# Two graph layers on one core: node tiles of 128 in place of 125, another order of the work in the preparation and the first edge stage, and no gathers of padding

## The chip, the cores and the metric

The kernel runs on one core of one Trainium2 chip. The metric is the device time of one execution in microseconds (us). A core has five engines with an instruction stream each: TensorE (PE, its weight loads are listed as PEld), VectorE (DVE), ScalarE (ACT), GpSimd (POOL) and SyncE (SP). They meet only at semaphores.

## What is computed

`x` has 6250 nodes of 256 values; 100,000 edges, sorted by `dst`, carry 64 values each. Two layers follow each other:

```python
h = relu(layernorm(x))
# layer 0, with a loop edge of zeros at every node
e   = relu(edge_attr @ ee_w1 + ee_b1) @ ee_w2 + ee_b2
agg = segment_sum(h[src] + e, dst)
y   = (1 + eps) * h + agg
y   = relu(ln(y @ w1 + b1)); y = relu(ln(y @ w2 + b2)); y = y @ w3 + b3
x   = x + relu(ln(h + y))
# layer 1, attention with 8 heads of 32, loops included
hp    = relu(layernorm(x)) @ W + b
s     = leaky_relu(h_src[src] + h_trg[dst])
alpha = exp(s - max(s)) / (segment_sum(exp(s - max(s)), dst) + 1e-10)
out   = x + segment_sum(hp[src] * alpha, dst)
```

Here `h_src` and `h_trg` are the sums of `hp * a_src` and `hp * a_trg` over a head. The second matrix of the edge network is applied after the sum over edges, per node.

## The kernel before

Nodes are cut into 50 tiles of 125 (`TN`, `NT`). Edges are cut into batches of 512 (`BE`), each in four chunks of 128; 100,000 edges fill 195.3 batches, and `NB` = 196. A table made in the preparation tells for every batch the first node tile that its `dst` reach and one past the last. A batch whose edges reach two tiles is called a straddling batch here; its sums are made twice, once for each tile. As `dst` is sorted, there is one such batch at every border between tiles.

The program has five parts.

- **`prepare`** normalises `x` in ten groups of five tiles (`PG`), writes the table of gathered rows to memory as a high and a low f16 half (`tab0`), turns the nodes' own part into `acc`, and makes the schedule. DVE does the statistics (L325, L328), the coefficients (L333, L334), the low halves (L346) and, in every second group, one half of the own part (L341); ACT normalises (L252), makes the high halves (L261) and takes the rest of the own part (L268); POOL adds a bias (L228); SP stores. `numbers`, `own_factors` and `schedule` are small DVE jobs that are slipped in between the groups. The buffers `tb` hold three groups, and `high` waits until a buffer has been stored.
- **`edges0`**, the first edge stage. For every batch POOL issues four gathers of 128 table rows (L550) into a ring of six buffers (`DEEP`). A round of POOL waits for `rows_free` once it is six batches ahead. The edge network of a batch goes through all engines: ACT copies the edge values to f16 (`eab`, L560, and `eah`, L561) and, after that, a part of the copy into a free corner of the network's own buffer in PSUM (L566); DVE makes the low part out of it (L665); PE multiplies (L612, L613: eight matmuls into `mlp_ps`); ACT takes the activation (`rh`, L587); DVE makes its low half (`rl`, L697). Then PE multiplies the gathered rows, `rh` and `rl` with a one-hot matrix of the batch's `dst` (L626, L627: 32 matmuls into `sum_ps`) and DVE adds the result to `acc` (L674). `hot` (L425) is the one-hot matrix. PE's body for batch b issues the edge network's matmuls of batch b+1 first and the sums of batch b after them; where b straddles, the second sums follow. PE loads its tile numbers from the table once in six batches, DVE once in four (both L436). After every sixteen batches ACT and DVE prepare one row of the node network's weights (L573, L576, L758, L749, L753).
- **`nodes`** runs the node network tile after tile, as a pipeline over five tiles, on f16 halves (L979); it writes the second table (`tab1`).
- **`edges1`**, the second edge stage, gathers `tab1` rows (L1561) into a ring of eight and sums them by one-hot matrices.
- **`finish`** divides by the sums of the exponents. Three of the ten groups of five tiles are scaled by ACT, head by head (L1934), the others by DVE.

In the first edge stage the order of the work is written out by hand. On ACT one turn is

```python
high_parts(1 - s)      # L560, L561, L566 of batch b+1
act.wait_ge(mlp_done, 1)
act.wait_ge(r_free, 1)
act.activation(rh...)  # L587 of batch b
```

`mlp_free` lets ACT write into the corner of the PSUM buffer once DVE has read that buffer's last batch; `r_free` lets ACT overwrite `rh` and is given by DVE's `used`, which stands after `add` and, behind a straddling batch, after `add_extra` (L687). DVE's function `advance` does the low part of batch b+1, the low half of batch b, the sums of batch b-1 and the one-hot matrix of batch b+1.

Of the kernel before, what the change touches and what calls it, by code (L numbers as in the profile page):

```python
# [32 lines left out]
P = 128  # L33
N, D, E, ED, H = 6250, 256, 100000, 64, 1024
TN = 125
NT = N // TN
# [5 lines left out]
NCH = NBP * CB  # L42
KH, KD = H // P, D // P
# [13 lines left out]
def build(nc, t, out):  # L57

    with ExitStack() as ctx:
        keep = Memory(nc, ctx)  # L60
        dram = {
            "tab0": nc.dram_tensor("tab0_scratch", (N, 2 * D), F16, kind="Internal").ap(),
            "tab1": nc.dram_tensor("tab1_scratch", (N, TW), F32, kind="Internal").ap(),
            "x1": nc.dram_tensor("x1_scratch", (N, D), F32, kind="Internal").ap(),
# [47 lines left out]
def prepare(nc, t, dram, sb):  # L112


    with ExitStack() as ctx:
# [3 lines left out]
        CH = NT // PG  # L119
        HALF = 112  # L120
        TB = 3
# [19 lines left out]
        tb = m.sb("tb", [TN, TB, PG, 2 * D], F16)  # L141
# [24 lines left out]
        tb_stored = [m.sem(f"tb_stored{s}") for s in range(TB)]  # L166
# [6 lines left out]
        def tiles(c):  # L173
            return slice(c * PG, (c + 1) * PG)
# [7 lines left out]
        def _(sp):  # L182
# [12 lines left out]
            def store(c):  # L195
                sp.wait_ge(tb_ready, c + 1)
                for rows in splits:
                    sp.dma_start(tb_v[rows, tiles(c), :], tb[rows, c % TB]).then_inc(tb_stored[c % TB], 16)

            for c in range(CH - 1):  # L200
                store(c)
            sp.wait_ge(sched_ready, 1)
            sp.dma_start(dram["spans"][1:NBP + 1].rearrange("(p j) c -> p (j c)", j=2), spans_sb[:].rearrange("p j c -> p (j c)")).then_inc(stored, 16)
            sp.dma_start(dram["spans"][0:1], spans_sb[0:1, 0, :]).then_inc(stored, 16)
            for p in range(2):
                line = dram["sched"][p]
                sp.dma_start(line[1:NBP + 1].rearrange("(p j) -> p j", j=2), sched_sb[:, p, :]).then_inc(stored, 16)
                sp.dma_start(line[0:1].unsqueeze(0), sched_sb[0:1, p, 0:1]).then_inc(stored, 16)
            store(CH - 1)
            sp.wait_ge(stored, 112)  # L210
            for s in range(TB):
                sp.wait_ge(tb_stored[s], 32 * len(range(s, CH, TB)))

        @block.gpsimd
        def _(pool):
# [8 lines left out]
            for c in range(CH):  # L224
# [3 lines left out]
                pool.tensor_tensor(ht[:, c % 2], acc[0:TN, tiles(c), 0:D], b2bc[:].unsqueeze(1).broadcast_to([TN, PG, D]),  # L228
# [6 lines left out]
        def _(act):  # L235
# [12 lines left out]
            def normalised(c):  # L248
                act.wait_ge(coef_ready, c + 1)
                for k in range(c * PG, (c + 1) * PG):  # L250
# [4 lines left out]
            def high(c):  # L255
                act.wait_ge(t_ready, c + 1)
# [4 lines left out]
                act.activation(tb[:, c % TB, :, 0:D], ht[:, c % 2], ACT.Copy).then_inc(hi_ready, 1)  # L261

            def own(c):
                if c == 0:
                    act.wait_ge(own_coef, 1)
                for j in range(KD) if on_act(c) else (0,):
                    act.wait_ge(own_done[j], c + 1)
                    act.activation(accT[:, tiles(c), j, 0:TN], own_ps[j][:, 0:PG, 0:TN], ACT.Identity,  # L268
# [5 lines left out]
            for c in range(CH + 3):  # L274
# [15 lines left out]
                if c == 5:  # L290
# [5 lines left out]
        def _(pe):  # L296
# [7 lines left out]
            for c in range(CH):  # L304
                pe.wait_ge(tb_ready, c + 1)
                for j in (1, 0):
                    if c:
                        pe.wait_ge(own_kept[j], c)
                    for k in range(PG):
# [6 lines left out]
        def _(dve):  # L316
# [5 lines left out]
            def stats(c):  # L322
                dve.wait_ge(ld_x[c], 32)
                for k in range(c * PG, (c + 1) * PG):
                    ins = dve.bn_stats(stat[:, k, :], acc[0:TN, k, 0:D])  # L325
                settled(ins)
                for k in range(c * PG, (c + 1) * PG):
# [9 lines left out]
            def own(c):  # L337
# [3 lines left out]
                dve.tensor_scalar(accT[:, tiles(c), 1, 0:TN], own_ps[1][:, 0:PG, 0:TN], eps2[:], own_off[:, 1:2],  # L341
                                  ALU.mult, ALU.add).then_inc(own_kept[1], 1)

            def low(c):
                dve.wait_ge(hi_ready, c + 1)
                settled(dve.tensor_tensor(tb[:, c % TB, :, D:2 * D], ht[:, c % 2], tb[:, c % TB, :, 0:D], ALU.subtract))  # L346
# [3 lines left out]
            def extremes(j):  # L350
                dve.wait_ge(ld_dst, 16)
                dve.tensor_reduce(ext[:, j:j + 1], drow[:, j, :], AX, ALU.min)
# [1667 lines left out]
```

## Time and profile before

| | us |
|---|---|
| median of the three runs (lowest to highest) | 3133.91 (3132.59 to 3136.23) |
| the profiled execution's own time | 3134.97 |
| its span, from the first to the last instruction | 3133.0 |
| PE busy | 2456.0 |
| DVE busy | 2233.0 |
| POOL busy | 1984.4 |
| ACT busy | 1592.6 |

The profiled execution lies 1.06 us above the median. The busy times are sums over four stages that differ in kind, so none of them is the bound by itself. The preparation ends at 89 us, the first edge stage at 1122 us, the node stage at 2089 us; the second edge stage and the last part take the rest. The start of an instruction in a timeline is the moment at which its waits were over.

### The profile page before, as it was taken

The numbers are of one execution on the slowest core, as the hardware profiler recorded it, in microseconds if no ns is written. First come the engines' busy times: TensorE is split into PE (matmuls) and PEld (weight loads), VectorE is DVE, ScalarE is ACT, GpSimd is POOL, SyncE is SP. The second block draws the span as 40 slices with busy tenths as digits, with TensorE's granted clock in tenths as the row PEclk, the third lists the DMA queues.
The fourth block names the chain that finished last, engine by engine and source line by source line (L and its number), as shares of the span: only waits on it lengthen the run. The fifth ranks groups of instructions, "written<-read, shape, count | busy, mean of one in ns | idle before, by whom it ended". The sixth has DMA issues, their size and how long they took to land. (4 is left out here: it accounts for less than half of the span.)

```text
span 3133.0 us, 88320 instructions
## 1 busy us (share of the span) xinstructions
PE 2456.0 (78%) x29338; PEld 2164.5 (69%) x29339; DVE 2233.0 (71%) x3932; ACT 1592.6 (51%) x3967; POOL 1984.4 (63%) x2094
## 2 busy tenths in 40 slices
PE   2677677777777779999999999938777777777773
PEld 2566666666666679999999999936555555555652
DVE  6566667776777657777777777758777777777777
ACT  6555555555555558888888888821111111111114
POOL 5677767777777724454544444437777777777772
PEclk9988889888899989999999999969888888988896
DMA  7555555555555510000000000026555555555554
GB/s 168 165 152 160 152 147 159 164 162 160 158 157 160 148 45 17 23 20 21 23 20 21 20 23 20 23 77 178 172 173 170 171 174 174 167 174 172 172 171 135
DMA packets 183986, 373.55 MB, mean 119 GB/s; under 512 B 42741, under 2 KB 93959, under 8 KB 183912
## 3 DMA queue, kind: packets, MB, share of 16 engines
q0 software_dynamic: 75552, 209.45, 23.7%
q1 hardware_dynamic: 107392, 162.37, 17.2%
q10 hardware_dynamic: 968, 0.87, 0.1%
q8 instruction: 31, 0.51, 0.1%
q14 instruction: 43, 0.35, 0.0%
HBM read 346.95 MB, written 25.80 MB: 119 GB/s over the span
## 5 line engine op out<-in xcount | busy, mean ns | idle before, releaser
L550 POOL DMA_INDIRECT rows<-tab_scratch,srcs x784 | 750.7, 958 | 264.4 <-issue 229.3
L1561 POOL DMA_INDIRECT a_rows<-tab_scratch,srcs x784 | 751.7, 959 | 250.9 <-issue 226.7
L1627 PE MATMUL sum_ps<-feat,a_hot 128*125 128x264 f32 x1960 | 599.0, 462 | 207.1 <-DVE feat L1720 98.1
L1627 PEld LDWEIGHTS sum_ps<-feat,a_hot 128*125 128x125 f32 x1960 | 417.6, 222 | 310.3 <-issue 117.8
L979 PE MATMUL z_ps<-ah,w 128*128 128x125 f16 x6400 | 555.1, 219 | 2.7 <-PEq L1075 2.6
L979 PE MATMUL z_ps<-al,w 128*128 128x125 f16 x3200 | 544.1, 218 | 0.0
L979 PEld LDWEIGHTS z_ps<-ah,w 128*128 128x128 f16 x6400 | 490.8, 97 | 3.5 <-issue 3.4
L1571 ACT ACTIVATE feat<-d 128x32 f32<-128x32 f32 x196 | 44.9, 229 | 827.2 <-DVE d L1716 580.5
L626 PE MATMUL sum_ps<-hot,rows 128*128 128x125 f16 x1960 | 356.1, 235 | 53.0 <-PEq L642 24.6
L612 PE MATMUL mlp_ps<-ewa,eab 128*128 128x256 f16 x788 | 213.9, 301 | 229.6 <-PEq L608 229.1
L626 PE MATMUL sum_ps<-hot,rh 128*128 128x125 f16 x1960 | 354.4, 234 | 0.0
L627 PE MATMUL sum_ps<-hot,rows 128*128 128x125 f16 x1960 | 354.3, 234 | 0.0
L627 PE MATMUL sum_ps<-hot,rl 128*128 128x125 f16 x1960 | 354.1, 234 | 0.0
L942 POOL TENSOR_TENSOR a<-a 128x500 f32<-128x500 f32 x100 | 153.8, 1538 | 310.8 <-POOLq L941 310.8
L1134 ACT ACTIVATE a<-z,pack 128x125 f32<-128x125 f32 x800 | 316.7, 483 | 44.2 <-ACTq L1132 44.2
L979 PEld LDWEIGHTS z_ps<-al,w 128*128 128x128 f16 x3200 | 315.6, 99 | 0.4
L612 PEld LDWEIGHTS mlp_ps<-ewa,eab 128*128 128x128 f16 x788 | 84.6, 107 | 265.1 <-issue 250.1
L626 PEld LDWEIGHTS sum_ps<-hot,rows 128*128 128x128 f16 x1960 | 205.9, 106 | 87.7 <-issue 84.2
L697 DVE SCALAR_TENSOR_TENSOR rl<-mlp_ps,rh 128x1024 f16<-128x1024 f32 x196 | 240.0, 1225 | 34.0 <-DVEq L696 29.6
L665 DVE TENSOR_TENSOR eab<-ea,mlp_ps 64x512 f16<-64x512 f32 x197 | 136.2, 691 | 164.4 <-DVEq L664 160.0
L566 ACT ACTIVATE mlp_ps<-eab 64x512 f32<-64x512 f16 x197 | 117.5, 597 | 250.7 <-ACTq L565 238.4
L1720 DVE TENSOR_TENSOR feat<-a_rows,p_ps 128x1024 f32<-128x1024 f32 x196 | 239.2, 1220 | 3.9 <-DVEq L1507 0.5
(220 smaller groups left out, 5938.7 us busy)
## 6 DMA issues: line engine op xcount, KB each, us to landing
ea<-edge_t SPq DMA_DIRECT2D x394, 128.0 KB
dstb<-dst_flat SPq DMA_DIRECT2D x98, 512.0 KB, 4.0
rows<-tab_scratch,srcs POOLq DMA_INDIRECT x784
a_rows<-tab_scratch,srcs POOLq DMA_INDIRECT x784
tab_scratch<-prow SPq DMA_DIRECT2D x50, 128.9 KB
hx<-x SPq DMA_DIRECT2D x50, 125.0 KB
x_scratch<-x SPq DMA_DIRECT2D x50, 125.0 KB
hs<-tab_scratch SPq DMA_DIRECT2D x50, 125.0 KB
```

The source lines that it names most:

```text
L550: pool.indirect_dma_start(rows[:, b % DEEP, k, :], None, dram["tab0"], bass.IndirectOffsetOnAxis(ap=srcs[:, c:c + 1], axis=0),).then_inc(r ...
L612: pe.matmul(mlp_ps[:, s, k, :], eab[:, s, e], ewa[:], start=True, stop=False)
L626: pe.matmul(to, high, rhs, start=(k == 0 and q == 0), stop=False, skip_group_check=True)
L627: ins = pe.matmul(to, low, rhs, start=False, stop=(k == CB - 1), skip_group_check=True)
L665: dve.tensor_tensor(eab[ED:P, s, :], ea[ED:P, s, :], high_ps[s], ALU.subtract).then_inc(ea_split, 1)
L697: dve.scalar_tensor_tensor(out=rl[:, s].rearrange("p k d -> p (k d)"), in0=mlp_ps[:, s].rearrange("p k d -> p (k d)"), scalar=0.0, in1=rh[ ...
L942: settled(pool.tensor_tensor(a[j][:, 0:4, :], a[j][:, 0:4, :], a[j][:, 4:8, :], ALU.add))
L979: ins = pe.matmul(out, lhs, rhs, start=(k == 0 and q == 0), stop=(k == n - 1 and q == 2))
L1134: ins = act.activation(a[j][:, k, :], z[j][:, k, :], ACT.Relu, bias=cols[be][:, k:k + 1], scale=cols[g][:, k:k + 1])
L1561: pool.indirect_dma_start(rows[:, b % DEEP, k, :], None, dram["tab1"], bass.IndirectOffsetOnAxis(ap=srcs[:, c:c + 1], axis=0),).then_inc(r ...
L1627: ins = pe.matmul(out[:], hot[:, h, k, :], feat[:, row, k, :], start=(k == 0), stop=(k == CB - 1))
L1720: return dve.tensor_tensor(feat[:, u, :, 0:D].rearrange("p k (h f) -> p k h f", h=HEADS), slot_of(slot)[:, :, 0:D].rearrange("p k (h f) -> ...
```

## The change

Nodes are now cut into 49 tiles of 128; the last has 106 nodes and 22 places without a node, and the inputs and tables are padded to 6272 rows. The preparation, the node stage and the last part count 49 tiles; the last group has four. In the second edge stage the extra partition that caught the padding edges is no longer needed, nor is a fiftieth tile's own loop term, which had been done ahead of the others. The two chunks that hold only padding (783 and 784 of 784) are no longer gathered. In the preparation `numbers` and `own_factors` stand ahead of the first statistics, DVE does the own part after the next statistics, the buffers for table groups lie in the node network's weights' room and number nine, the last bias is added by DVE, and the schedule is made and stored before the last groups. In the first edge stage ACT takes the activation of batch b before the copies of batch b+1, and DVE takes the low half of batch b before the low part of batch b+1.

```diff
-TN = 125
-NT = N // TN
+TN = P
+NT = -(-N // TN)
+TAIL = N - (NT - 1) * TN
+FILLED = -(-E // P)
...
# edges0, POOL (edges1 alike)
-                for k in range(CB):
+                for k in range(min(CB, FILLED - CB * b)):
...
# edges0, ACT
                 act.activation(eab[:, s, :], ea[:, s, :], ACT.Copy).then_inc(eab_chain, 1)
-                act.activation(eah[0:ED, s, :], ea[0:ED, s, :], ACT.Copy).then_inc(eah_done, 1)
                 act.wait_ge(mlp_free, 1)
...
                 act.activation(high_ps[s], eab[ED:P, s, :], ACT.Copy).then_inc(ea_high, 1)
+                act.activation(eah[0:ED, s, :], ea[0:ED, s, :], ACT.Copy).then_inc(eah_done, 1)
...
                 for u in range(RING):
                     s = u % 2
-                    high_parts(1 - s)
                     act.wait_ge(mlp_done, 1)
...
                     act.activation(rh[:, s]...).then_inc(r_high, 1)
+                    high_parts(1 - s)
...
# edges0, DVE, advance
                     extra_hot(b - 1, end - 1)
+                    low_activations(s)
+                    low_parts(1 - s)
                     add(1 - s, lo)
-                    low_parts(1 - s)
-                    low_activations(s)
                     main_hot(b + 1, 1 - s, following)
                     add_extra(end - 1)
...
                 with dve.Else():
+                    low_activations(s)
                     low_parts(1 - s)
-                    low_activations(s)
                     add(1 - s, lo)
...
# prepare, DVE
+            numbers()
+            own_factors()
             stats(0)
             for c in range(CH + 3):
                 if c < CH:
                     coefficients(c)
-                if 3 <= c < CH:
-                    own(c - 3)
+                if c == CH:
+                    last_sum()
                 if 2 <= c < CH + 2:
                     low(c - 2)
...
                 if c + 1 < CH:
                     stats(c + 1)
-                if c == 0:
-                    own_factors()
-                if c == 1:
-                    numbers()
+                if c >= 3:
+                    own(c - 3)
...
# prepare, ACT
-                    act.wait_ge(tb_stored[c % TB], 32 * (c // TB))
+                    act.wait_ge(first_stored, 32)
...
# finish, ACT
-                for k in range(i * FB, (i + 1) * FB):
+                for k in range(i * FB, min((i + 1) * FB, NT)):
```

**ACT in the first edge stage.** One turn and the start of the next before the change (`mlp_ps<-eab` is the copy into the corner of PSUM):

```order
L560 ACTIVATE eab<-ea 128x512 [waits ea_ready1]
L561 ACTIVATE eah<-ea 64x512
L566 ACTIVATE mlp_ps<-eab 64x512 [waits mlp_free,eab_chain]
L587 ACTIVATE rh<-mlp_ps 128x1024 [waits mlp_done,r_free]
L560 ACTIVATE eab<-ea 128x512 [waits ea_ready0]
```

And now:

```order
L607 ACTIVATE rh<-mlp_ps 128x1024 [waits mlp_done,r_free]
L582 ACTIVATE eab<-ea 128x512 [waits ea_ready0]
L587 ACTIVATE mlp_ps<-eab 64x512 [waits mlp_free,eab_chain]
L588 ACTIVATE eah<-ea 64x512
L607 ACTIVATE rh<-mlp_ps 128x1024 [waits mlp_done,r_free]
```

The activation `rh` of a batch moved from behind the three copies of the next batch to ahead of them, and the copy into `eah` moved behind the copy into PSUM.

**DVE in the first edge stage, behind a straddling batch.** From the extra one-hot matrix to the addition of the extra sums, before:

```order
L425 SCALAR_TENSOR_TENSOR hot<-dsts,negbase,e_iota_ps 128x500
L674 ISA [waits e_chain,sum_done]
L674 TENSOR_TENSOR acc<-acc,sum_ps 128x4x125
L665 TENSOR_TENSOR eab<-ea,mlp_ps 64x512 [waits ea_high]
L697 SCALAR_TENSOR_TENSOR rl<-mlp_ps,rh 128x1024 [waits r_high]
L425 ISA
L425 SCALAR_TENSOR_TENSOR hot<-dsts,negbase,e_iota_ps 128x500
L687 ISA [waits xsum_done]
L687 TENSOR_TENSOR acc<-acc,sum_ps 128x4x125
```

And now:

```order
L447 SCALAR_TENSOR_TENSOR hot<-dsts,negbase,e_iota_ps 128x512
L718 SCALAR_TENSOR_TENSOR rl<-mlp_ps,rh 128x1024 [waits r_high]
L686 TENSOR_TENSOR eab<-ea,mlp_ps 64x512 [waits ea_high]
L695 ISA [waits e_chain,sum_done]
L695 TENSOR_TENSOR acc<-acc,sum_ps 128x512
L447 ISA
L447 SCALAR_TENSOR_TENSOR hot<-dsts,negbase,e_iota_ps 128x512
L708 ISA [waits xsum_done]
L708 TENSOR_TENSOR acc<-acc,sum_ps 128x512
```

The low half `rl` and the low part `eab` moved ahead of the instruction that waits for the sums of the batch before (`sum_done`), and `rl` now stands first.

**DVE at the start of the preparation.** Before:

```order
L384 MEMSET lneps 128x1
L325 BN_STATS stat<-acc 125x6 [waits p_dve_chain,ld_x0]
L325 BN_STATS stat<-acc 125x6 x4
L328 BN_AGGR mv_ps<-stat 125x2 [waits p_dve_chain]
L328 BN_AGGR mv_ps<-stat 125x2 x4
```

And now:

```order
L406 MEMSET lneps 128x1
L377 TENSOR_SCALAR ident<-idiag 128x128 [waits p_dve_chain,iotas]
L378 TENSOR_SCALAR ident<-idiag 128x128
L379 CAST iota<-icol 128x128
L380 CAST negbase<-ineg 128x49
L381 CAST nodeid<-inode 128x49
L382 CAST thr<-ithr 128x48
L386 TENSOR_SCALAR ecol<-ecol 128x2 [waits p_dve_chain,ld_eps]
L387 TENSOR_SCALAR eps<-eps 128x1
L388 TENSOR_SCALAR ecol<-ecol,eps 128x2 [waits p_dve_chain]
L389 TENSOR_SCALAR eps<-eps 128x1 [waits p_dve_chain]
L339 BN_STATS stat<-acc 128x6 [waits p_dve_chain,ld_x0]
```

The six instructions of `numbers` and the four of `own_factors` moved from behind the statistics of the second and third group to ahead of the first group's.

## Rows read from the trace of the kernel before

**Rows 1.** The first three stages; columns: us, busy of each engine, clock, DMA, GB/s.

```profile
0.00:89.00 89.00, 25.29 (x208) 21.68 (x209) 59.21 (x159) 53.84 (x90) 41.97 (x23) 1.00 0.69 163
89.00:1122.00 1033.00, 752.04 (x9416) 665.28 (x9416) 715.71 (x923) 562.31 (x811) 751.63 (x785) 0.89 0.54 156
1122.00:2089.00 967.00, 927.19 (x14416) 919.31 (x14416) 673.98 (x1169) 796.75 (x2151) 438.52 (x502) 0.98 0.07 22
```

**Rows 2.** Gather instructions of both edge stages, by source line; start times in us.

```profile
L550 POOL DMA_INDIRECT rows<-tab_scratch,srcs x784: 947/953/1744, 90.1 to 1104.1; - x196
...
L1561 POOL DMA_INDIRECT a_rows<-tab_scratch,srcs x784: 952/957/1322, 2089.6 to 3079.5; - x196
```

**Rows 3.** Timeline, batches 95 to 98; columns: start, length in us, engine, line, operation.

```profile
603.39 0.22 PE L626 MATMUL sum_ps<-hot,rows 128*128 128x125 f16 x1 [0.25 <-PEq L642]
...
605.11 0.22 PE L627 MATMUL sum_ps<-hot,rl 128*128 128x125 f16 x1
...
605.97 0.63 ACT L560 ACTIVATE eab<-ea 128x512 f16<-128x512 f32 x1 [0.89 <-ACTq L559]
...
608.66 0.27 PE L612 MATMUL mlp_ps<-ewa,eab 128*128 128x256 f16 x1 [3.33 <-PEq L608]
...
609.26 0.60 ACT L566 ACTIVATE mlp_ps<-eab 64x512 f32<-64x512 f16 x1 [2.14 <-ACTq L565]
...
609.91 1.02 ACT L587 ACTIVATE rh<-mlp_ps 128x1024 f16<-128x1024 f32 x1
...
610.00 0.69 DVE L665 TENSOR_TENSOR eab<-ea,mlp_ps 64x512 f16<-64x512 f32 x1 [1.61 <-DVEq L664]
...
611.09 1.23 DVE L697 SCALAR_TENSOR_TENSOR rl<-mlp_ps,rh 128x1024 f16<-128x1024 f32 x1 [0.40 <-DVEq L696]
```

**Rows 4.** Timeline of ACT at the end of a round of sixteen batches.

```profile
539.44 1.02 ACT L587 ACTIVATE rh<-mlp_ps 128x1024 f16<-128x1024 f32 x1 [0.74 <-ACTq L586]
540.48 1.15 ACT L573 ACTIVATE centred<-w,wneg 128x1024 f32 x1
541.82 1.06 ACT L576 ACTIVATE w<-centred 128x1024 f32 x1 [0.19 <-ACTq L575]
```

**Rows 5.** Timeline, batch 101, matmuls twice as long.

```profile
629.28 0.69 DVE L665 TENSOR_TENSOR eab<-ea,mlp_ps 64x512 f16<-64x512 f32 x1 [2.26 <-DVEq L664]
...
630.26 0.36 PE L612 MATMUL mlp_ps<-ewa,eab 128*128 128x256 f16 x1 [4.94 <-PEq L608]
...
632.32 1.02 ACT L587 ACTIVATE rh<-mlp_ps 128x1024 f16<-128x1024 f32 x1
```

**Rows 6.** Register loads of the schedule in the first edge stage, by source line.

```profile
L436 PEldq TENSOR_LOAD <-st x66: 1003/1466/1662, 98.2 to 1105.4; - x66
```

**Rows 7.** Timeline of DVE in the same place.

```profile
538.21 0.67 DVE L687 TENSOR_TENSOR acc<-acc,sum_ps 128x500 f32 x1
...
543.16 1.24 DVE L758 TENSOR_TENSOR w<-centred,w 128x1024 f32 x1
...
548.27 0.69 DVE L665 TENSOR_TENSOR eab<-ea,mlp_ps 64x512 f16<-64x512 f32 x1 [2.25 <-DVEq L664]
```

**Rows 8.** Timeline, the first matmul of the first edge stage.

```profile
97.72 0.37 PE L612 MATMUL mlp_ps<-ewa,eab 128*128 128x256 f16 x1 [11.56 <-PEq L608]
```

**Rows 9.** Timeline of the preparation, POOL and DVE.

```profile
6.98 5.42 POOL L222 MEMSET acc<- 128x6400 f32 x1
...
8.82 1.73 DVE L325 BATCH_NORM_STATS2 stat<-acc 125x6 f32<-125x256 f32 x5 [7.94 <-DMA acc<-x]
...
21.82 2.98 DVE L362 CAST thr<-ithr 128x49 f32<-128x49 int32 x1
...
74.99 3.96 DVE L346 TENSOR_TENSOR tb<-ht,tb 125x1280 f16<-125x1280 f32 x1 [0.75 <-ACT tb L261]
```

**Rows 10.** One operation of each node tile, by source line.

```profile
L1128 ACT ACTIVATE a<-z x50: 1029/1037/1041, 1131.5 to 2023.2; 128x1000 f32<-128x1000 f32 x50
```

**Rows 11.** Timeline of ACT in the last stage.

```profile
3101.53 25.54 ACT L1934 ACTIVATE acc<-acc,f_g 125x32 f32<-125x32 f32 x120 [3.71 <-DVEq L1970]
```

More of the change, by code:

```diff
@@ L165, in prepare @@
         own_kept = [m.sem(f"own_kept{j}") for j in range(KD)]
-        tb_stored = [m.sem(f"tb_stored{s}") for s in range(TB)]
+        first_stored, tb_stored, t_last = m.sem("first_stored"), m.sem("tb_stored"), m.sem("t_last")
         dve_chain = m.sem("p_dve_chain")
@@ L223, in _ @@
             pool.wait_ge(ld_b2, 16)
-            for c in range(CH):
+            for c in range(LASTC):
                 pool.wait_ge(norm_ready, c + 1)
@@ L249, in normalised @@
                 act.wait_ge(coef_ready, c + 1)
-                for k in range(c * PG, (c + 1) * PG):
+                for k in range(c * PG, c * PG + count(c)):
                     h = acc[0:TN, k, 0:D]
@@ L255, in high, with own @@
             def high(c):
-                act.wait_ge(t_ready, c + 1)
+                if c < LASTC:
+                    act.wait_ge(t_ready, c + 1)
+                else:
+                    act.wait_ge(t_last, 1)
                 if c >= TB:
-                    act.wait_ge(tb_stored[c % TB], 32 * (c // TB))
+                    act.wait_ge(first_stored, 32)
                     for j in range(KD):
                         act.wait_ge(own_done[j], c - TB + 1)
-                act.activation(tb[:, c % TB, :, 0:D], ht[:, c % 2], ACT.Copy).then_inc(hi_ready, 1)
-            def own(c):
+                act.activation(tb[:, c % TB, 0:count(c), 0:D], ht[:, c % 2, 0:count(c)], ACT.Copy).then_inc(hi_ready, 1)
+            def own(c, parts):
                 if c == 0:
                     act.wait_ge(own_coef, 1)
-                for j in range(KD) if on_act(c) else (0,):
+                for j in parts:
                     act.wait_ge(own_done[j], c + 1)
-                    act.activation(accT[:, tiles(c), j, 0:TN], own_ps[j][:, 0:PG, 0:TN], ACT.Identity,
+                    act.activation(accT[:, tiles(c), j, 0:TN], own_ps[j][:, 0:count(c), 0:TN], ACT.Identity,
                                    bias=own_off[:, j:j + 1], scale=eps2[:]).then_inc(own_kept[j], 1)
@@ L286, in _ @@
                 if c >= 3:
-                    own(c - 3)
+                    own(c - 3, (1,) if on_act(c - 3) else (0,))
                 if c + 1 < CH:
                     deviation(c + 1)
-                if c == 5:
+                if c >= 3 and on_act(c - 3):
+                    own(c - 3, (0,))
+                if c == 6:
                     act.wait_ge(eb_split, 1)
@@ L308, in _ @@
                         pe.wait_ge(own_kept[j], c)
-                    for k in range(PG):
+                    for k in range(count(c)):
                         out = own_ps[j][:, k, 0:TN]
@@ L323, in stats @@
                 dve.wait_ge(ld_x[c], 32)
-                for k in range(c * PG, (c + 1) * PG):
+                for k in range(c * PG, c * PG + count(c)):
                     ins = dve.bn_stats(stat[:, k, :], acc[0:TN, k, 0:D])
                 settled(ins)
-                for k in range(c * PG, (c + 1) * PG):
+                for k in range(c * PG, c * PG + count(c)):
                     ins = dve.bn_aggr(mv[:, k, :], stat[:, k, :])
@@ L633, in _, with body @@
             edge_mlp(0)
-            def body(tiles, i, u):
+            def body(tiles, i, u, last=False):
                 s = u % 2
@@ L643, in body @@
                 pe.sem_inc(mlp_free, 1)
-                pe.wait_ge(rows_ready[u], 16 * CB * (i + 1))
+                pe.wait_ge(rows_ready[u], 16 * (CB * (i + 1) - (NB * CB - FILLED if last else 0)))
                 sums(sum_ps[:, s, :], s, u, s).then_inc(sum_done, 1)
@@ L885, in bodies @@
         def bodies(eng, body):
-            first, last = 4, NT - 2
+            first, last = 4, NT - 3
+            assert (last - first) % 2 == 0
             for i in range(first):
@@ L1558, in _ @@
                     pool.wait_ge(rows_free, b - DEEP + 1)
-                for k in range(CB):
+                for k in range(min(CB, FILLED - CB * b)):
                     c = CB * b + k
@@ L1915, in _ @@
         def _(sp):
-            out_v = out.rearrange("(t p) c -> p t c", p=TN)
+            whole = (NT - 1) * TN
+            out_v = out[0:whole].rearrange("(t p) c -> p t c", p=TN)
             for i in range(steps):
-                tiles = slice(i * FB, (i + 1) * FB)
+                tiles = slice(i * FB, min((i + 1) * FB, NT - 1))
                 sp.wait_ge(out_ready, i + 1)
@@ L1921, in _ @@
                     sp.dma_start(out_v[rows, tiles, :], acc[rows, tiles, 0:D]).then_inc(out_stored, 16)
-            sp.wait_ge(out_stored, 32 * steps)
+            sp.dma_start(out[whole:N], acc[0:TAIL, NT - 1, 0:D]).then_inc(out_stored, 16)
+            sp.wait_ge(out_stored, 32 * steps + 16)
         @block.scalar
```

129 lines of the change are left out of this document (70 added, 59 removed).

## The prediction

> **What bounds the kernel now.** I read the windows by stage first, because the stages differ in kind. The preparation takes 89 us, the first edge stage 1033, the node stage 967 with PE busy in 927 of them [rows 1]; what is left of the span (3133.0) is 1044 us. No engine is full in the first edge stage: PE is busy in 752 of 1033 us. Then I read the gathers [rows 2]. In the second edge stage 784 of them start over 989.9 us, one each 1.264 us, with little else to do. In the first edge stage they start over 1014.0 us, one each 1.295. At the second stage's pace a batch of four could come every 5.06 us; it came every 5.18. So the gathers are close to being the pace, but the computation holds them up a little. The reader should see there a stage with a slack of some 2% in either direction: a loop of more than 5.06 us per batch on the compute side lengthens it, and a shorter one gains 784 × (1.295 − 1.264) = 24 us and a part of the 18 that follow the last gather (1104.1 to 1122).
>
> Then I read the timeline of single batches. Now, ACT copies the edge values of batch b+1 (L560, L561, L566) while PE and ACT are still busy with batch b; the next network's inputs are ready early, and the activation `rh` comes after them. This is a pipeline of two batches. The example shows also what disturbs it: the last sums matmul of a batch starts at 605.11, and PE's next network matmul only at 608.66, 3.55 us later, of which PE stood idle for 3.33 [rows 3]. PE loads its tile numbers in between.
>
> **The first edge stage: a serial loop.** After the change ACT does `rh` of b first and then copies for b+1. `rh` of b waits for the network's matmuls of b, these for the low part of b on DVE, this for ACT's copy into PSUM of b, and this stands in ACT's queue behind `rh` of b−1. The dependence goes round once per batch, and nothing in it overlaps:
>
> - network matmuls to `rh`: 608.66 to 609.91, 1.25 us [rows 3];
> - `rh` to ACT's next instruction: 539.44 to 540.48, 1.04 us [rows 4];
> - copy `eab`: 0.63 long [rows 3], and the next instruction of ACT that waits for the one before stands 0.19 more [rows 4]: 0.82 us;
> - copy into PSUM to low part: 609.26 to 610.00, 0.74 us [rows 3];
> - low part to network matmul: 629.28 to 630.26, 0.98 us [rows 5].
>
> The sum is 4.83 us at 2.4 GHz. What lies beside it: `rl` of b starts 1.18 us behind `rh` and lasts 1.23 [rows 3], 2.41 in all, and the low part is due 1.04 + 0.82 + 0.74 = 2.60 behind it, so `rl` hides; the sums of one batch take 603.39 to 605.33 = 1.94 [rows 3], and with the network's matmuls, which are over within the 1.25, they fit in 4.83, and the columns from 125 to 128 hide with them. `eah` and the additions hide too. 196 × 4.83 = 947, and 4 for the tail. Alone this is under 5.06, and the gathers would decide. But a serial loop never catches up: whatever holds one batch up is added in full, where the old pipeline took it beside the copies. I count four such things.
>
> (a) PE's registers: 66 loads of 1.47 us in pairs [rows 6], 32 times in the stage. PE's own loop is there the network, the sums, the loads: from the first sums matmul to the next network 603.39 to 608.66 = 5.27 [rows 3], and ahead of it the network, about 0.89 as an estimate (the 1.25 without the last matmul's 0.27 and some 0.09 for the signal): 6.16 instead of 4.83, +1.3. In 14 of the 32 the batch or the one before straddles (counted from `dst` with tiles of 128; 7 with tiles of 125), which puts 1.72 more on PE (603.39 to 605.11): +3.0. 18 × 1.3 + 14 × 3.0 = 65 us.
>
> (b) The other 34 of the 48 straddling batches (49 before): `r_free` comes only behind `add_extra`, 538.21 + 0.67 to `rh` at 539.44, 0.56 us [rows 4, 7], and `add_extra` waits for second sums. About 0.9 each: 31 us. Nearest bounds: nothing, and 1.72.
>
> (c) Twelve weight rows: from DVE's product on a row to the next low part pass 543.16 to 548.27, 5.1 us [rows 7], with ACT's two instructions 2.4 [rows 4] ahead. The old pipeline covered much of it. I take 5.0 each: 60 us; the lower bound is ACT's 2.4, 29 us.
>
> (d) The clock. It was 0.89 on average [rows 1], so (1 − 0.89)/0.5 = 22% of the stage at 1.2 GHz. There, network to `rh` is 630.26 to 632.32 = 2.06 [rows 5], 0.81 more than at 2.4 GHz. I keep a fifth: 0.2 × 196 × 0.81 = 31 us; bounds 0 and 159.
>
> The stage begins 8.7 us ahead of its first network matmul (89 to 97.72 [rows 8]). Sum: 8.7 + 951 + 65 + 31 + 60 + 31 = 1147, against 1033: **+114 us**. With the least that I can defend of (a) to (d), 93 us ((a) 32 × 1.3 = 42, (c) 29, (d) 22, (b) nothing), it is +20; with (a) and (b) at 1.72 more for each straddle, (c) with 2.4 more and (d) at half of the stage, about +200. I take the middle terms, because each has its row in this stage.
>
> **The preparation.** `thr` takes 2.98 beside POOL's work, and `low` 3.96 once, where a buffer was late [rows 9]; both leave the chain of groups. The own part goes behind the next statistics and the schedule's stores start before the last groups; no row prices these, and I put them at one `low`, 4. Against it, `numbers` and `own_factors` now stand ahead of the first statistics, which started at 8.82, and POOL's memset runs until 12.40 [rows 9]; they could be held until then, +3.6. That is −7, from −14 (nothing held, both moves worth twice as much) to +4 (only the hold counts). The DVE instructions there that are long for their size end with POOL's, as the rows suggest. The Trainium skill ("GPSIMD Engine Reference", § 1. Specifications) says that GpSimd shares an SBUF interface with VectorE; by it the ten small instructions would be drawn out under the memset, and the preparation would come out at about +3 instead of −7, the kernel at 3244.
>
> **Nodes.** 50 tiles pass at (2023.2 − 1131.5)/49 = 18.2 us [rows 10], PE being the bound. One tile fewer is −18.2; if each tile cost 128/125 as much, 49 × 18.6 = 913 against 910, +3. PE does most work in blocks of 512 columns, and a part by the tile's columns. I take −3.
>
> **Second edge stage and finish.** 782 gathers of 1.264 instead of 784 [rows 2]: −2.5. ACT scales 14 tiles by 8 heads, 112 operations instead of 120, each 25.54/120 = 0.213 [rows 11]: −1.7; bounds 0 and −3.
>
> **Sum.** 114 − 7 − 3 − 2.5 − 1.7 = +99.8. The profiled execution has 3134.97 and lies 1.06 above the median: 3134.97 + 99.8 − 1.06 = 3233.7, **3234 us**.
>
> **The rivals.** *A, faster: the gathers set the pace.* If most of (a) to (d) falls in time in which the batch waits for its rows anyway, a mean batch takes under 5.06 us, and (782 × 1.264 = 988) + 9 us of start and tail make the stage 997, −36; with the other gains (−14) the kernel takes about 3084. The place is the loop's 4.83, the point is disturbances of less than 0.23 × 196 = 45 us in all. For it speaks that the loop alone is under the gathers' pace; against it that (a) alone, which the trace shows bare in the old order, makes 42 to 65.
> *B, nothing:* the lower bounds of (a) to (d) hold: +20 − 14 = +6 on the median: 3140. With (d) at nothing too it is 22 less, with the preparation's gain gone 8 more.
> *C, slower still: the clock falls more.* In a loop with longer pauses for PE the low clock's share may go from a fifth to half or more: 0.3 × 196 × 0.81 = 48 more by this loop alone, and more with the sums: about 3300. Rows show that both levels occur in this stage [rows 1, 5]. The Trainium skill ("TensorE: Matmul & The Clock Gate", "Loop structure matters more than you think") says that PE work in dense stretches keeps the clock and long waits between lose it; by it the change, which spaces the stretches out, leads to case C.
> *D:* that a step doesn't do what is said is excluded by the order lists, which show ACT's and DVE's new order.
>
> **How the numbers follow.** A 0.15, B 0.12, C 0.06, the forecast 0.67, with its own range 3165 to 3290. Within 0.2% (6 us, about what a measurement of this kernel can tell from no change) lies only a part of B, which I spread from 3100 to 3165: 0.05 there, 0.05 below it and 0.02 above. Faster: A and that lower part, 0.20. Slower: the forecast, C and the upper part, 0.75. The range, 3095 to 3300, takes in the forecast's own range, the whole of B, the near third of A and the near half of C; two thirds of A (0.10), the far half of C (0.03) and 0.05 of the forecast remain outside.
>
> **What would show it.** Right: after the change the windows by stage give the first edge stage about 1147 us; ACT's `rh` of consecutive batches stands 4.8 us apart where nothing disturbs; POOL waits long for free rows. Wrong: POOL without waits, gathers one each 1.27 us, and a stage under 1010 (case A); or a spacing of `rh` well off 4.83. In the node stage 49 tiles at 18.5 us or so; in the preparation the first statistics at about 12 us instead of 8.82.

## The result, and the profile after the change

The changed kernel takes 3264.86 us (median of four runs, 3262.53 to 3267.17) against 3133.25 us before (four runs): a ratio of 1.0421, 95% interval 1.0403 to 1.0439. That is +131.6 us where +100 was forecast. The profiled execution has 3262.53 us and a span of 3260.7, 127.7 more than the span before.

The windows by stage of the changed kernel, with the columns of [rows 1]:

```profile
0.00:80.00 80.00, 24.44 (x204) 21.63 (x205) 63.80 (x158) 52.45 (x89) 38.27 (x22) 1.00 0.74 181
80.00:1257.00 1177.00, 797.89 (x9384) 723.99 (x9384) 733.52 (x921) 568.20 (x811) 751.04 (x783) 0.84 0.47 137
1257.00:2218.00 961.00, 916.69 (x14128) 885.57 (x14128) 674.75 (x1147) 790.38 (x2108) 445.92 (x492) 0.98 0.07 22
2218.00:3260.00 1042.00, 746.83 (x5278) 561.17 (x5278) 783.36 (x1676) 176.34 (x900) 748.47 (x783) 0.84 0.58 170
```

The first edge stage has grown from 1033 to 1177 us, and its clock has fallen from 0.89 to 0.84; every other stage is shorter. From here on, the stage is taken from its first gather to the end of its last addition: 90.1 to 1121.9 before (1031.8 us) and 81.1 to 1257.0 now (1175.9), +144.1. The other parts: the preparation −9.0 (first gather at 81.1, at 90.1 in [rows 2]), the node stage 961.7 instead of 967.7, −6.0, the second edge stage with the finish 1042.1 instead of 1043.5, −1.4. The sum is +127.7.

The gathers, by source line, with what POOL waited for in the first stage (us, times):

```profile
L572 POOL DMA_INDIRECT rows<-tab_scratch,srcs x782: 947/953/1996, 81.1 to 1230.1; - x196
...
  DVEq L699: 184.4, 74
...
L1584 POOL DMA_INDIRECT a_rows<-tab_scratch,srcs x782: 952/957/1081, 2218.6 to 3204.1; - x196
```

POOL waited 184 us for `rows_free` (L699). In the second stage gathers still start one each 1.262 us ((3204.1 − 2218.6)/781). So the transfers did not become slower; POOL was held up by the computation.

An undisturbed round in the first edge stage, in the timeline of ACT, DVE and PE:

```profile
247.92 1.02 ACT L607 ACTIVATE rh<-mlp_ps 128x1024 f16<-128x1024 f32 x1 [1.77 <-ACTq L606]
...
249.10 1.22 DVE L718 SCALAR_TENSOR_TENSOR rl<-mlp_ps,rh 128x1024 f16<-128x1024 f32 x1 [1.36 <-DVEq L717]
...
249.57 0.60 ACT L587 ACTIVATE mlp_ps<-eab 64x512 f32<-64x512 f16 x1
...
250.35 0.69 DVE L686 TENSOR_TENSOR eab<-ea,mlp_ps 64x512 f16<-64x512 f32 x1
...
251.34 0.27 PE L633 MATMUL mlp_ps<-ewa,eab 128*128 128x256 f16 x1 [1.84 <-PEq L629]
...
252.60 1.02 ACT L607 ACTIVATE rh<-mlp_ps 128x1024 f16<-128x1024 f32 x1 [1.77 <-ACTq L606]
```

The round from `rh` to `rh` is 252.60 − 247.92 = 4.68 us, and 80 of 195 rounds lie between 4.67 and 4.70; before, the shortest round was 3.36. The reader can follow two ways round. By ACT: `rh` to the copy into PSUM 1.65, to the low part 0.78. By DVE: `rh` to `rl` 1.18, to the low part 1.25. Both make 2.43, and after them come the low part to the network, 0.99, and the network to `rh`, 1.26. The low part starts 0.03 us behind the end of `rl` (250.32): the two ways tie.

A round behind a border between tiles (the first matmul of the batch's sums, the extra one-hot matrix, the first matmul of the second sums, the network, the extra addition, `rh`):

```profile
252.23 0.22 PE L647 MATMUL sum_ps<-hot,rows 128*128 128x128 f16 x1
...
253.81 0.75 DVE L447 SCALAR_TENSOR_TENSOR hot<-dsts,negbase,e_iota_ps 128x512 f16<-128x512 f32 x1 [1.39 <-issue]
...
255.52 0.31 PE L647 MATMUL sum_ps<-hot,rows 128*128 128x128 f16 x1
...
257.43 0.27 PE L633 MATMUL mlp_ps<-ewa,eab 128*128 128x256 f16 x1
...
257.83 0.69 DVE L708 TENSOR_TENSOR acc<-acc,sum_ps 128x512 f32 x1
...
259.07 1.02 ACT L607 ACTIVATE rh<-mlp_ps 128x1024 f16<-128x1024 f32 x1 [3.57 <-ACTq L606]
```

Network matmuls would have been due at 251.34 + 4.68 = 256.02. PE does the second sums just ahead of the network, which starts at 257.43, 1.41 us late. In this round the extra one-hot matrix is ready at 253.81 + 0.75 = 254.56, but PE is then still at the batch's own sums, which run at the low level of the clock, 1.2 GHz (0.51 in the stretch below):

```profile
252.30:255.70 3.40, 3.40 (x35) 3.40 (x34) 2.00 (x3) 2.77 (x4) 2.49 (x4) 0.51 0.65 180
```

From the start of the first to the start of the last matmul they take 3.18 us, and 1.73 in most of the 48 rounds behind borders. In 37 of the 48 the order is the other way: PE has done the batch's own sums and stands still for 0.7 us or more until the extra one-hot matrix is there, which DVE mostly makes behind its loads. Then `rh` waits for the extra addition (257.83 + 0.69, and 0.55 more) until 259.07; 1.26 behind the network it would have started at 258.69, so this is 0.38 us. The round shown has 6.47 us, 1.79 more than 4.68. Where PE's loads fall into the same round, such rounds have 9.2 us on average (10 of them), with a weight row 11.4 (6), with both 14.1 (4).

### The profile page after: what moved, and what is told of

Same layout as the page of the kernel before. It is cut to its first block and busy times, and to the rows that moved or that the text cites. A ratio compares the mean times of both kernels' runs of the same rounds, so it can differ in the third digit from the quotient of the medians.

```text
span 3260.7 us, 87292 instructions
## 1 busy us (share of the span) xinstructions
PE 2485.8 (76%) x28994; PEld 2192.4 (67%) x28995; DVE 2255.4 (69%) x3901; ACT 1587.4 (49%) x3907; POOL 1983.7 (61%) x2079
## 5 line engine op out<-in xcount | busy, mean ns | idle before, releaser
L1648 PE MATMUL sum_ps<-feat,a_hot 128*128 128x264 f32 x1952 | 593.4, 461 | 219.1 <-PEq L1535 104.4
L1648 PEld LDWEIGHTS sum_ps<-feat,a_hot 128*128 128x128 f32 x1952 | 424.2, 226 | 317.8 <-issue 190.3
L1000 PE MATMUL z_ps<-ah,w 128*128 128x128 f16 x6272 | 544.2, 220 | 2.0 <-PEq L1096 1.8
L1000 PE MATMUL z_ps<-al,w 128*128 128x128 f16 x3136 | 533.3, 220 | 0.0
L607 ACT ACTIVATE rh<-mlp_ps 128x1024 f16<-128x1024 f32 x196 | 200.3, 1022 | 569.5 <-ACTq L606 536.7
L647 PE MATMUL sum_ps<-hot,rows 128*128 128x128 f16 x1952 | 379.4, 247 | 72.1 <-PEq L670 72.1
L647 PE MATMUL sum_ps<-hot,rh 128*128 128x128 f16 x1952 | 379.2, 247 | 0.0
L648 PE MATMUL sum_ps<-hot,rows 128*128 128x128 f16 x1952 | 379.2, 247 | 0.0
L648 PE MATMUL sum_ps<-hot,rl 128*128 128x128 f16 x1952 | 378.8, 247 | 0.0
L1155 ACT ACTIVATE a<-z,pack 128x128 f32<-128x128 f32 x784 | 312.3, 484 | 40.0 <-ACTq L1153 40.0
L447 DVE SCALAR_TENSOR_TENSOR hot<-dsts,negbase,e_iota_ps 128x512 f16<-128x512 f32 (+1 forms) x245 | 181.6, 743 | 75.6 <-issue 73.5
```

Source lines behind the costliest of these rows:

```text
L447: return dve.scalar_tensor_tensor(out=out, in0=at, scalar=negbase[:, bass.ds(tile, 1)], in1=iota_ps.unsqueeze(1).broadcast_to([P, CB, TN]) ...
L607: act.activation(rh[:, s].rearrange("p k d -> p (k d)"), mlp_ps[:, s].rearrange("p k d -> p (k d)"), ACT.Relu).then_inc(r_high, 1)
L647: pe.matmul(to, high, rhs, start=(k == 0 and q == 0), stop=False, skip_group_check=True)
L648: ins = pe.matmul(to, low, rhs, start=False, stop=(k == CB - 1), skip_group_check=True)
L1000: ins = pe.matmul(out, lhs, rhs, start=(k == 0 and q == 0), stop=(k == n - 1 and q == 2))
L1155: ins = act.activation(a[j][:, k, :], z[j][:, k, :], ACT.Relu, bias=cols[be][:, k:k + 1], scale=cols[g][:, k:k + 1])
```

## The experiments

The theory (S): the new order closes a serial loop of 4.7 us per batch, and this loop, not the gathers, is the pace of the stage. The rivals: with tiles of 128 borders fall into the same batches as DVE's loads (P); DVE's order, with the extra sums behind the low parts, costs the time (D); gathers set or slow the stage (G). Twelve kernels were run. The stage lengths are from the first gather to the last addition of one execution, the profiled one. 1 to 6 were timed four times each, 7 to 12 once, so these have no interval.

| kernel | whole, us | first edge stage, us |
|---|---|---|
| before | 3133.3 | 1031.8 |
| changed | 3264.9 | 1175.9 |
| 1: changed, old order | 3115.0 | 1023.5 |
| 2: before, new order | 3260.6 | 1151.2 |
| 3: changed, old order on ACT only | 3249.1 | 1161.3 |
| 4: changed, old order on DVE only | 3280.0 | 1187.0 |
| 5: changed, PE's loads behind the network | 3255.5 | 1170.4 |
| 6: as 1, PE's loads behind the network | 3091.6 | 998.3 |
| 7: changed, half the gathers | 3260.6 | 1168.0 |
| 8: as 1, half the gathers | 3114.1 | 1017.9 |
| 9: changed, no second sums | 3083.8 | 996.0 |
| 10: changed, no weight rows | 3208.8 | 1117.8 |
| 11: as 8, no second sums | 2852.1 | 755.3 |
| 12: as 7, no second sums | 3084.9 | 992.2 |

**1: the old order back, everything else as changed.**

```diff
 # ACT, high_parts
                 act.activation(eab...).then_inc(eab_chain, 1)
+                act.activation(eah...).then_inc(eah_done, 1)
...
                 act.activation(high_ps[s]...).then_inc(ea_high, 1)
-                act.activation(eah...).then_inc(eah_done, 1)
 # ACT, turn
+                    high_parts(1 - s)
                     act.wait_ge(mlp_done, 1)
...
                     act.activation(rh...).then_inc(r_high, 1)
-                    high_parts(1 - s)
 # DVE, advance at a border
                     extra_hot(b - 1, end - 1)
-                    low_activations(s)
-                    low_parts(1 - s)
                     add(1 - s, lo)
+                    low_parts(1 - s)
+                    low_activations(s)
 # DVE, advance elsewhere
-                    low_activations(s)
                     low_parts(1 - s)
+                    low_activations(s)
                     add(1 - s, lo)
...
```

> The changed kernel with the order of before on ACT and on DVE in the first edge stage; tiles of 128, preparation and gathers as changed. Serial loop (theory S): the first edge stage falls from 1177 us to about 1030, the whole to about 3118 us, below the kernel before, as the other parts gained some 15. Rival P (with 128 nodes a tile holds 2048 edges on average, four batches, so that nearly every border falls into the batches where DVE also loads its tile numbers): that stays, and the stage keeps some 50 us of its 144, 3165 us.

3115.03 us, a ratio to before of 0.9947 (0.9930 to 0.9963). The stage's row:

```profile
81.30:1104.80 1023.50, 735.08 (x9384) 648.74 (x9384) 720.79 (x918) 560.22 (x811) 751.87 (x782) 0.91 0.55 157
```

The stage is 8 us shorter than before, at a clock of 0.91, and the kernel 19 faster. So the order makes the whole loss, and what was changed beside it gains. P's 50 us are not there.

**2: the new order alone in the kernel before**, the reverse of the diff above.

> The kernel before with the changed order on ACT and DVE in the first edge stage alone; tiles of 125, preparation and gathers of before. S: spacing of rh 4.7 us where nothing disturbs, the stage about 1160, the whole about 3255 to 3280 us. P: the order costs only some 90 us, 3220 us, because borders and loads meet only by chance with tiles of 125.

3260.60 us, ratio 1.0406 (1.0386 to 1.0426): in S's range. The order costs 1151.2 − 1031.8 = 119 us of the stage with tiles of 125 and 1175.9 − 1023.5 = 152 with tiles of 128; of the whole, by the medians, it costs 127 and 150. Some 23 to 33 us thus belong to the order and the tiles together. In the changed kernel 44 of the 48 rounds behind borders are also rounds with DVE's loads, with tiles of 125 it is 12 of 49; a tile of 128 nodes has 2048 edges on average, four batches. That this is the reason was not tried by itself.

**3: the old order on ACT only; 4: on DVE only.** Each has its half of the diff of 1.

> The changed kernel with the order of before on ACT alone; DVE as changed. S: the loop is opened by ACT's copies alone, the same time as with both orders put back, within 10 us. Rival D (DVE's order, its extra sums behind the low parts, costs the time): like the changed kernel, about 3250 to 3265 us.

> The changed kernel with the order of before on DVE alone; ACT as changed. S: the loop stays serial, 3265 us or a little more, since low parts now stand ahead of the low half without need. D: about 3120 us.

3249.13 us for the first (1.0365, 1.0347 to 1.0382), 3280.04 for the second (1.0472, 1.0455 to 1.0490). S as I had put it, with ACT alone, falls for 3, where D's figure came, and D falls for 4. A round of each shows why. Old order on ACT:

```profile
247.28 0.60 ACT L588 ACTIVATE mlp_ps<-eab 64x512 f32<-64x512 f16 x1 [0.29 <-ACTq L587]
...
248.11 1.02 ACT L609 ACTIVATE rh<-mlp_ps 128x1024 f16<-128x1024 f32 x1 [0.23 <-ACTq L608]
...
249.29 1.22 DVE L719 SCALAR_TENSOR_TENSOR rl<-mlp_ps,rh 128x1024 f16<-128x1024 f32 x1 [1.57 <-DVEq L718]
...
250.55 0.69 DVE L687 TENSOR_TENSOR eab<-ea,mlp_ps 64x512 f16<-64x512 f32 x1
...
251.54 0.27 PE L634 MATMUL mlp_ps<-ewa,eab 128*128 128x256 f16 x1 [0.43 <-PEq L630]
...
252.98 1.00 ACT L609 ACTIVATE rh<-mlp_ps 128x1024 f16<-128x1024 f32 x1
```

ACT's copy into PSUM is done early, and yet the low part of the next batch waits: DVE has it behind `rl`, `rl` waits for `rh`. The round shown is 4.87 us, the commonest one 4.68. Old order on DVE:

```profile
250.68 1.02 ACT L607 ACTIVATE rh<-mlp_ps 128x1024 f16<-128x1024 f32 x1 [1.75 <-ACTq L606]
...
252.34 0.60 ACT L587 ACTIVATE mlp_ps<-eab 64x512 f32<-64x512 f16 x1
...
253.09 0.69 DVE L686 TENSOR_TENSOR eab<-ea,mlp_ps 64x512 f16<-64x512 f32 x1 [1.46 <-DVEq L685]
...
254.08 0.27 PE L633 MATMUL mlp_ps<-ewa,eab 128*128 128x256 f16 x1 [1.46 <-PEq L629]
...
255.34 1.02 ACT L607 ACTIVATE rh<-mlp_ps 128x1024 f16<-128x1024 f32 x1 [1.74 <-ACTq L606]
```

Here `rl` is out of the way, and the low part waits for ACT's copy. The round is 4.66 us. Each of the two moves closes the loop by itself, at the same length; both have to go.

**5 and 6: PE's loads behind the network**, in the changed kernel and in 1.

```diff
-            def body(tiles, i, u, last=False):
+            def body(tiles, i, u, last=False, n=DEEP):
                 s = u % 2
                 edge_mlp(1 - s)
+                if u == 0:
+                    tiles.extend(tiles_of(nc, PE, table, DEEP * i, n))
...
-                tiles = tiles_of(nc, PE, table, DEEP * i, DEEP)
+                tiles = []
```

> The changed kernel, but PE loads its tile numbers behind the network of the group's first batch instead of ahead of it. If the serial loop is the pace (S), each of the 32 loads, which made a round of rh about 2.5 us longer than 4.68, now lies mostly beside the loop's steps on ACT and DVE: some 50 us less, about 3215 us. If gathers or something else set the pace (rival G): no change, 3265 us.

> The same move of the loads in the changed kernel with the old order on ACT and DVE. If that one's first edge stage (1023 us) is close to the gathers' pace (988 us), at most 25 to 30 us go: 3090 to 3105 us. If it is still the pace of the computation alone, 50 us or more would go.

3255.52 us (1.0405, 1.0388 to 1.0423) and 3091.55 us (0.9883, 0.9867 to 0.9900). For 5 my 50 us were wrong; the stage lost 5.5. One such place in PE's timeline:

```profile
164.18 0.27 PE L633 MATMUL mlp_ps<-ewa,eab 128*128 128x256 f16 x1
...
168.05 0.29 PE L647 MATMUL sum_ps<-hot,rows 128*128 128x128 f16 x1 [2.82 <-PEq L665]
...
171.27 0.27 PE L633 MATMUL mlp_ps<-ewa,eab 128*128 128x256 f16 x1
```

From one network to the next PE now needs 171.27 − 164.18 = 7.09 us, because network, loads and sums stand one behind the other on PE and the sums run at the low level for a part (clock 0.50 from 168 to 171 us). In the changed kernel the first round behind a load, borders and rows apart, had 7.2 us on average; here the second has 6.8. The wait moved one batch on. In 6 the same move gave 25 us of the stage. Its gathers:

```profile
L572 POOL DMA_INDIRECT rows<-tab_scratch,srcs x782: 949/953/1535, 81.3 to 1066.1; - x196
```

They start one each (1066.1 − 81.3)/781 = 1.261 us, the pace of the second stage: of the versions that make all sums, only this one has reached the gathers' floor. It beats the kernel before by 1.2%.

**7 and 8: half the gathers**, in the changed kernel and in 1.

```diff
+            pool.memset(rows[:, :, CB // 2:CB, :], 0.0).then_inc(ones_ready, 1)
...
-                for k in range(min(CB, FILLED - CB * b)):
+                for k in range(CB // 2):
...
```

> The changed kernel with two of four gathers of each batch in the first edge stage; the other two chunks of rows are zeros, so their share of the sums is left out. S: the loop is the pace, the first edge stage keeps its 1176 us within 15. G (gathers set or slow it): well under 1130 us.

> The same with the old order on ACT and DVE. If gathers set its pace for a good part, the stage falls from 1023 us to 900 to 960; if the computation alone does, it stays at 1010 to 1025.

The stage has 1168.0 and 1017.9 us, 8 and 6 less than with all gathers. Of this, 5 us come from the zeros: they are written ahead of the first gather, which starts at 86.6 instead of 81.1 and 81.3. The stage ends 2.5 and 0.4 us sooner. G falls. The second also shows that the gathers do not hold the old order, near as its pace is to theirs.

**9: no second sums at borders; 10: no weight rows.**

```diff
 # 9, PE and DVE
-                with pe.If(end > lo + 1):
-                    with pe.Fori(lo + 1, end):
...
-                with dve.If(end > lo + 1):
...
-                with dve.Else():
 # 10, ACT, DVE and SP
-                row(r)
-                row_mean(r)
-                row_low(r)
-                load_row(r + 1)
```

> The changed kernel without the second sums of a batch that reaches two tiles, in the first edge stage (that part of the sums is left out). By the terms of the prediction (31 us, and 24 in the loads' term) the stage falls by 55 us to about 1120; by the longer rounds of rh that stand two batches behind a border in the changed kernel's trace (some 2 to 2.7 us each) by 100 to 130, to about 1060.

> The changed kernel without the twelve weight rows in the first edge stage (the node network's weights are zeros). By the prediction's term the stage falls by 60 us to about 1116; by the trace (about 4.5 us for a row) by 55.

The stage without second sums, and below without weight rows:

```profile
81.10:1077.10 996.00, 683.70 (x7848) 617.35 (x7848) 671.13 (x822) 568.10 (x811) 748.52 (x782) 0.84 0.55 161
```

```profile
81.30:1199.10 1117.80, 769.98 (x9384) 700.99 (x9384) 701.68 (x882) 544.25 (x787) 765.37 (x783) 0.87 0.48 138
```

Without second sums the stage is 180 us shorter, above even the larger expectation. But 9 leaves out more than the second sums. Nothing reads the last tile of a batch any more, and PE reads no tile number at all; the loads of these numbers are gone too. Below are the changed kernel's loads, and then 9's:

```profile
L458 DVEq TENSOR_LOAD <-st x101: 309/815/833, 81.8 to 1254.1; - x101
L458 PEldq TENSOR_LOAD <-st x66: 1004/1467/1663, 88.1 to 1235.0; - x66
```

```profile
L458 DVEq TENSOR_LOAD <-st x51: 329/807/830, 81.9 to 1075.4; - x51
```

So the 180 us are the price of borders, of PE's loads and of half of DVE's loads together. The rounds of the two traces, batch by batch, divide them: the 34 rounds with a border alone are 2.0 us longer in the changed kernel (69 us), the 17 with PE's loads alone 2.1 (35 us), the 14 with both 4.6 (65 us); the other 130 together make 9. Without weight rows the stage is 58 us shorter, as expected, and the clock is 0.87 instead of 0.84.

**11 and 12: half the gathers and no second sums**, in 1 and in the changed kernel, the edits of 7 and 9 together; PE's loads and half of DVE's are gone here too.

> The changed kernel with the old order on ACT and DVE, with half the gathers (the other rows are zeros) and without the second sums at borders, so that neither gathers nor borders hold its first edge stage. If borders cost the old order about as much as the new one (theory: the change is the longer loop alone), the stage falls from 1018 us to 800 to 880: 196 rounds of 3.4 to 3.9 us, and weight rows and loads. If the old order took the borders beside its copies (the prediction's view), it stays over 960.

> The changed kernel with half the gathers and without the second sums. The serial loop is the floor: 196 x 4.68 = 917 us, weight rows 58 and a little for loads and clock: 975 to 1000, hardly under the 996 us that it took with all gathers. If gathers held that run up, clearly less than 975.

The stage of 11, and below of 12:

```profile
86.50:841.80 755.30, 611.78 (x7848) 521.23 (x7848) 652.96 (x821) 553.88 (x808) 373.58 (x392) 0.95 0.49 144
```

```profile
86.40:1078.60 992.20, 681.20 (x7848) 613.81 (x7848) 669.46 (x820) 566.26 (x808) 373.27 (x392) 0.85 0.39 109
```

Freed of half the gathers, of borders and of PE's loads, the old order needs 755 us and the new one 992: 237 us, weight rows and what is left of DVE's loads included. 9, with all its gathers, has 996; that it is no longer than 12 says that gathers did not hold 9 up either, though they start one each (1066.7 − 81.1)/781 = 1.262 us there. The loop is 196 × 4.68 = 917 us in the new order, and with the 58 of the weight rows 975 of the 992 are accounted for. In the old order a bare round, in the timeline of 11, has 3.36 us, from `rh` at 247.73 to `rh` at 251.09:

```profile
247.73 1.00 ACT L611 ACTIVATE rh<-mlp_ps 128x1024 f16<-128x1024 f32 x1
...
247.94 0.69 DVE L684 TENSOR_TENSOR eab<-ea,mlp_ps 64x512 f16<-64x512 f32 x1 [0.40 <-DVEq L683]
...
248.76 0.63 ACT L584 ACTIVATE eab<-ea 128x512 f16<-128x512 f32 x1
...
248.93 0.27 PE L636 MATMUL mlp_ps<-ewa,eab 128*128 128x256 f16 x1 [0.40 <-PEq L632]
...
250.55 0.60 ACT L590 ACTIVATE mlp_ps<-eab 64x512 f32<-64x512 f16 x1 [0.64 <-ACTq L589]
...
251.09 1.00 ACT L611 ACTIVATE rh<-mlp_ps 128x1024 f16<-128x1024 f32 x1
```

The next batch's low part starts 0.21 us behind `rh`, beside it, and not 2.43 behind, and its network is on PE before `rh` has been over for long.

Borders and loads together cost 1017.9 − 755.3 = 263 us in the old order and 1168.0 − 992.2 = 176 in the new. So the new order does give something back there, 87 us, and 237 − 87 = 150 is what is seen between 7 and 8. By rounds, 8 against 11 and 7 against 12: a border alone costs 3.3 us in the old order and 2.1 in the new, PE's loads alone 2.8 and 2.1, both 5.5 and 4.7. That they cost the old order more because they break a pipeline of two batches is only argued.

## Why the prediction was right, and where it was not

The direction, the range and the likeliest case held, and the sum came to three quarters of what was measured. By its steps:

- **A serial loop.** Right, and it is the cause: putting the order back takes 152 us off the stage. The forecast of 4.83 us was 0.15 too long: `rh` to the copy into PSUM takes 1.65, not 1.04 + 0.82 = 1.86.
- **"`rl` hides".** This failed. It was set against ACT's way of 2.60 us with 2.41; in the run both ways have 2.43. The step saw one loop where there were two, and with either move alone the loop is closed (3 and 4).
- **"Alone this is under 5.06, and the gathers would decide."** This held as far as the runs go: in 9, with the weight rows but without borders and PE's loads, the gathers start at their own pace of 1.262 us.
- **"Where the old pipeline took it beside the copies."** This failed. The old order bears borders and loads as well, with 263 us even more than the new one with 176 (8 and 11, 7 and 12). Its mean round lay near the gathers' pace by coincidence; with half the gathers it stays (8), and without borders and PE's loads the stage falls to 755 us (11). So the computation did not grow by disturbances that the old order had hidden, but by 237 us of longer rounds less 87 that borders and loads cost less. The old order without borders and PE's loads but with all gathers was not run; by the 998 us of 6, as an estimate, the gathers would hold it there, and the longer loop would be hidden, as the text had it.
- **(a) to (d).** Forecast 187 us in all. (c) weight rows: 60 forecast, 58 measured. (a) and (b) together, PE's loads and borders: 65 + 31 = 96 forecast, 180 measured, half of DVE's loads among them (9); these are the terms that were mis-sized. By rounds, loads alone make 2.1 us each where 1.3 was forecast, borders alone 2.0 where 0.9, both 4.6 where 3.0, so that the border is the term that was mis-sized most. Its 0.9 had counted the wait of `rh` for the extra addition, which is 0.38 us in the round shown; 1.41 come from PE, which has the second sums ahead of the next network, there with the batch's own sums at the low level before them. Moving the loads recovers only 5.5 us, as the wait moves with them (5). (d) the clock: 0.84 on average is (1 − 0.84)/0.5 = 32% at 1.2 GHz against 22% before. What this costs by itself was not separated. The networks, from which (d) was reckoned, were hit no more often than before: 33 of the 197 needed over 1.2 us from the start of the first to the start of the last matmul instead of 0.78, and 36 before. The low level comes more often in the sums, as in the border round shown.
- **The sum of the stage**, 1147 forecast for 1177. The size came near partly by luck: the loop's 951 was 30 too many and the clock's 31 have no run that shows them, against 84 too few in (a) and (b).
- **Preparation** −7 forecast, −9.0 measured. The first statistics started at 13.96 us instead of 8.82, later than the 12 that were forecast; the last rows of this document show what held them. The Trainium skill ("GPSIMD Engine Reference", § 1. Specifications) names contention only with VectorE's instructions in a 2-port mode or with two inputs in SBUF, which the prediction left out; in the trace two of the ten small instructions are drawn out and the other eight follow them. The +3 us worked out from that sentence did not come: holds of the same kind, such as `thr`'s 2.98 us inside the chain [rows 9], went at the same time. What each move gave was not separated.
- **Nodes** −3 forecast, −6.0 measured; second edge stage and finish −4.2 forecast, −1.4 measured: its gathers end 4.5 us sooner relative to its start, and what follows the last gather takes 3.1 more. That the last gather is now one of real edges, with its work behind it, would explain this, but it was not tried.
- **Rivals.** A needed rounds under 5.06 us; the mean was 5.94. C, the clock, went its way by a part: the Trainium skill ("TensorE: Matmul & The Clock Gate", "Loop structure matters more than you think") and the stage's mean clock, 0.89 before and 0.84 now, agree in direction, but the low level did not reach half of the stage.

What is open: how much of 144 us the low clock makes by itself, what borders cost without the loads that went with them in 9, 11 and 12, and why borders and loads cost the old order more.

## What to carry to other kernels

When two engines hand a batch back and forth, follow the dependence once round through every engine's queue, in program order: an instruction for batch b+1 that stands behind one for batch b on any of them closes the loop, and undoing it on one engine shows little (15 us either way here) while a second still closes it. A mean pace that agrees with a transfer's pace is no proof that the transfer sets it; halve the transfer and look. And price a rare case (a border) by its whole round, from `rh` to `rh`, and not by the one wait that is easiest to see. Where a part is left out to price it, count the instructions in both traces: what only that part had read is gone with it, and is in the price.

## What was not expected of the hardware

In the changed preparation two small instructions of DVE start while POOL clears `acc`, and last until it is done (the first of them is shown):

```profile
1.62 5.21 POOL L230 MEMSET acc<- 128x6144 f32 x1
...
1.69 10.59 DVE L377 TENSOR_SCALAR ident<-idiag 128x128 f32<-128x128 int32 x1 [0.81 <-POOL ithr L229]
...
6.78 5.42 POOL L231 MEMSET acc<- 128x6400 f32 x1
...
12.27 0.21 DVE L379 CAST iota<-icol 128x128 f16<-128x128 int32 x1
...
13.96 1.73 DVE L339 BATCH_NORM_STATS2 stat<-acc 128x6 f32<-128x256 f32 x5
```

The same instruction in the kernel before, when no memset ran:

```profile
21.25 0.21 DVE L357 TENSOR_SCALAR ident<-idiag 128x128 f32<-128x128 int32 x1
```

So 128 columns took 10.59 us under the memsets and 0.21 without them, while the second memset took 5.42 us in both kernels [rows 9]. Not every instruction of DVE is held: the kernel before did its first five statistics beside the same memset in 1.73 us [rows 9], as long as the five above, which had no memset beside them.
